# Last attention of a four-layer graph network: VectorE's weights and decays moved from SBUF to PSUM, row sums in six banks

## What is computed

```python
h = (x @ W_att).reshape(n, H, D)                 # H = 8, D = 64
a_src = jnp.einsum('nhc,hc->nh', h, att_src)
a_dst = jnp.einsum('nhc,hc->nh', h, att_dst)
e = a_src[src] + a_dst[dst]
e = jnp.where(e > 0, e, SLOPE * e)
m = jax.ops.segment_max(e, dst, num_segments=n)
e = jnp.exp(e - m[dst])
s = jax.ops.segment_sum(e, dst, num_segments=n)
alpha = e / (s[dst] + SM_EPS)
msg = alpha[:, :, None] * h[src]
out = jax.ops.segment_sum(msg, dst, num_segments=n)
```

## Time and profile before

| what | value |
|---|---|
| median of 3 runs | 5495.73 us (5489.99 to 5499.63) |
| the profiled execution's own time | 5500.16 us |
| its span, first to last instruction | 5498.4 us |
| POOL busy | 3629.3 us (66%) |
| DVE busy | 4024.2 us (73%) |
| PE busy | 2485.3 us (45%) |
| ACT busy | 1267.6 us (23%) |

### The profile page before, as it was taken

The page is one execution under the profiler, slowest core; times in us unless marked ns, Lnnn a source line. Parts: engine busy times, 40 slices in busy tenths (PEclk is TensorE's granted clock), DMA queues, the critical chain, the costliest instruction groups (busy, mean ns, idle before and its releaser), DMA issues.

```text
span 5498.4 us, 51371 instructions
## 1 busy us (share of the span) xinstructions
PE 2485.3 (45%) x13080; PEld 1698.2 (31%) x13080; DVE 4024.2 (73%) x7076; ACT 1267.6 (23%) x4432; POOL 3629.3 (66%) x3780
## 2 busy tenths in 40 slices
PE   1697100102112133333332335559882677777765
PEld 0572000101112123232232324537771233323324
DVE  9877888887886578787887878745552676677677
ACT  0000000000000011111111111110002777777761
POOL 2777777777777777777777777430006777777743
PEclk6555555555555555555555555569996888888886
DMA  7212111121222232323222233237761222222222
GB/s 251 56 54 58 49 55 46 48 71 42 62 53 66 50 82 80 83 79 83 75 79 82 80 83 89 79 97 254 235 200 30 76 86 86 78 85 86 79 73 67
DMA packets 392241, 476.93 MB, mean 87 GB/s; under 512 B 216403, under 2 KB 252309, under 8 KB 384838
## 3 DMA queue, kind: packets, MB, share of 16 engines
q1 hardware_dynamic: 136422, 279.67, 15.0%
q0 software_dynamic: 114832, 133.36, 10.7%
q10 hardware_dynamic: 140752, 61.28, 4.0%
HBM read 294.77 MB, written 179.24 MB: 86 GB/s over the span
## 4 chain that ended last, share of the span: by engine, by line
POOL 51%; issue 20%; DVE 15%; PE 9%; DMA 4%; ACT 0%; POOLq 0%; ACTq 0%; DVEq 0%; SPq 0%
POOL arena L794 36%; POOL rec_dram L751 12%; PE acc L2267 4%; DVE OHX L1547 3%; PE pw L2255 2%; DMA V<-in_edge_attr_dram 1%; DVE oh L1557 1%; DVE arena L1569 1%; DVE V L1589 1%; DVE arena L1573 1%; POOL own_dram L771 1%; DVE sc L1574 1%; DMA rec_dram<-V,rowst 1%; DVE oh L1547 1%; PE acc L2209 1%
## 5 line engine op out<-in xcount | busy, mean ns | idle before, releaser
L794 POOL DMA_INDIRECT arena<-tab_dram,jst x2592 | 2527.3, 975 | 778.6 <-issue 772.7
L751 POOL DMA_INDIRECT rec_dram<-V,rowst x784 | 840.3, 1072 | 231.4 <-issue 221.4
L2201 PE MATMUL pw<-OHX 128*128 128x128 bf16 x1632 | 207.7, 307 | 800.0 <-DVE OHX L1547 798.7
L2209 PE MATMUL acc<-arena,oh 128*128 128x64 f32 x1952 | 420.7, 415 | 254.0 <-DVE oh L1557 254.0
L2209 PEld LDWEIGHTS acc<-arena,oh 128*128 128x128 f32 x1952 | 410.9, 325 | 268.2 <-issue 268.2
L982 ACT ACTIVATE arena<-arena,ew 128x64 f32<-128x64 f32 x1728 | 417.8, 333 | 31.2 <-PE acc L2303 31.2
L982 ACT ACTIVATE OHX<-arena,ew 128x64 f32<-128x64 f32 x1728 | 417.8, 333 | 2.5
L2303 PE MATMUL acc<-OHX,ident 128*128 128x512 f32 x432 | 252.9, 751 | 364.2 <-ACT OHX L982 361.6
L2201 PEld LDWEIGHTS pw<-OHX 128*128 128x128 bf16 x1632 | 154.7, 139 | 850.7 <-DVE OHX L1547 850.7
L1569 DVE TENSOR_TENSOR arena<-arena,pt 128x1024 f32<-128x1024 f32 x108 | 131.9, 1221 | 386.4 <-DMA arena<-tab_dram,jst 384.3
L744 POOL TENSOR_TENSOR pdum<-pdum 128x1 f32<-128x1 f32 x197 | 53.4, 271 | 440.7 <-DVE arena L1844 199.2
(11 more groups left out here) (578 smaller groups left out, 6272.6 us busy)
## 6 DMA issues: line engine op xcount, KB each, us to landing
arena<-tab_dram,jst POOLq DMA_INDIRECT x2592
arena<-rec_dram SPq DMA_DIRECT2D x122, 288.0 KB, 3.7
mt_dram<-oh ACTq DMA_DIRECT2D x272, 128.0 KB, 1.7
rows_dram<-V SPq DMA_DIRECT2D x27, 1056.0 KB, 4.0
rows_dram<-arena SPq DMA_DIRECT2D x27, 1056.0 KB, 4.3
V<-in_edge_attr_dram ACTq DMA_DIRECT2D x97, 256.0 KB
oh<-mt_dram SPq DMA_DIRECT2D x42, 512.0 KB, 4.7
OHX<-mt_dram SPq DMA_DIRECT2D x38, 512.0 KB, 4.6
```

Of the source, the lines that this page charges most:

```text
L751: gp.indirect_dma_start(rec[:, :], bass.IndirectOffsetOnAxis(ap=rowst[:, q, k:k + 1], axis=0), recst[:, q, k, :], None).then_inc(S[f"scat{ ...
L794: gp.indirect_dma_start(hd.G[:, a.r, j, :], None, table[:, :], row_of(jst[:, a.r, j:j + 1])).then_inc(S[f"rows{a.r}"], 16)
L2201: last = nc.tensor.matmul(unit_bank(c.slot)[:, k // 2 * P:(k // 2 + 1) * P], mones[c.slot][:, 0, k, :], mones[c.slot][:, 1, k, :], start=k ...
L2209: last = nc.tensor.matmul(o, roh[:, c.q, k, :], RG[:, c.r, k, 0:D], start=False, stop=True, skip_group_check=True)
```

## The change

The weights that DVE uses (the first four edges of each pair of rows, 128 numbers a partition) and the decays (64 numbers) now stand in PSUM, in the two banks of `pt`, one for even and one for odd blocks. ACT writes them there: L973 puts its result there, and a new instruction takes the exponential of the 128 arguments a second time, ahead of the one over all 256 in SBUF, which ACT's own weighting and the sums of the weights still need; DVE's wait for `dx` counts one more. Block 26 keeps both in SBUF.

Since `pt` no longer holds row sums, rows 6 and 7 of a block use the banks of rows 2 and 3. So PE must have had rows 2 and 3 read before it sums pair 3 of the same block, and the states are made two pairs later in DVE's order relative to the pair they belong to, but partly inside their own block: after weighting pairs 0 and 1 come the states of pairs 2 and 3 of the block before, after weighting pairs 2 and 3 those of pairs 0 and 1 of the same block. Block 25 leaves only pairs 2 and 3 to the part outside the loop.

```diff
--- before.py
+++ after.py
@@ -526,7 +526,20 @@
 
         def row_bank(f):
 
-            return acc[:, f * 512:(f + 1) * 512] if f < 4 else (accw, pu, pt[:, 0:512], pt[:, 512:1024])[f - 4]
+            return (accw, pu)[f - 4] if 4 <= f < 6 else acc[:, f % 4 * 512:f % 4 * 512 + 512]
+
+        def last_block(a):
+
+            return isinstance(a.g, int) and a.g == NB3 - 1
+
+        def decays3(a):
+
+            return dc[:, a.q] if last_block(a) else pt[:, a.q * 512 + 128:a.q * 512 + 128 + RB * H3].rearrange("p (f h) -> p f h", h=H3)
+
+        def weights_of(a):
+
+            return (ew[:, a.q].rearrange("p (f k h) -> p f k h", k=8, h=H3)[:, :, 0:8 - VA] if last_block(a) else
+                    pt[:, a.q * 512:a.q * 512 + 128].rearrange("p (f k h) -> p f k h", k=8 - VA, h=H3))
 
         @block.sync
         def _(sp):
@@ -970,10 +983,14 @@
             def weights3(a):
 
                 act.wait_ge(S["de"], 2 * a.g + 1)
-                A.activation(dc[:, a.q], dc[:, a.q], ACT.Exp).then_inc(S["dx"], 1)
+                A.activation(decays3(a), dc[:, a.q], ACT.Exp).then_inc(S["dx"], 1)
                 act.wait_ge(S["de"], 2 * a.g + 2)
+                if not last_block(a):
+                    A.activation(weights_of(a), ew[:, a.q].rearrange("p (f k h) -> p f k h", k=8, h=H3)[:, :, 0:8 - VA], ACT.Exp
+                                 ).then_inc(S["dx"], 1)
+                    act.wait_ge(S["dx"], 3 * a.g + 2)
                 A.activation(ew[:, a.q], ew[:, a.q], ACT.Exp).then_inc(S["dx"], 1)
-                act.wait_ge(S["dx"], 2 * a.g + 2)
+                act.wait_ge(S["dx"], 3 * a.g + 2 + (not last_block(a)))
                 for f in range(RH):
                     slot_taken3(act, a, f)
                     for k in range(8 - VA, 8):
@@ -1860,8 +1877,8 @@
                     before = SO3[1 - half][:, RH - 1] if row == 0 else SO3[half][:, row - 1]
                     o = SO3[half][:, row]
                     byh = lambda u: u[:, 0:H3 * D].rearrange("p (h d) -> p h d", h=H3)
-                    st(V.tensor_tensor(byh(o), byh(before), dc[:, c.q, f].unsqueeze(2).to_broadcast([P, H3, D]), ALU.mult), wait=False)
-                    st(V.tensor_tensor(o[:, 512:520], before[:, 512:520], dc[:, c.q, f], ALU.mult))
+                    st(V.tensor_tensor(byh(o), byh(before), decays3(c)[:, f].unsqueeze(2).to_broadcast([P, H3, D]), ALU.mult), wait=False)
+                    st(V.tensor_tensor(o[:, 512:520], before[:, 512:520], decays3(c)[:, f], ALU.mult))
                     v.wait_ge(S["dsm"], RH * c.g + f // 2 + 1)
                     V.tensor_tensor(o[:, 0:512], o[:, 0:512], row_bank(f), ALU.add).then_inc(S["dpb"], 1)
                     v.wait_ge(S["dpb"], RB * c.g + f + 1)
@@ -1879,8 +1896,7 @@
                     t = f * 8 + k
                     ins = V.tensor_tensor(V3r[vslot[f]][:, k * 512:(k + 2) * 512].rearrange("p (k h d) -> p k h d", h=H3, d=D),
                                           G3[:, a.r, t:t + 2, 0:D].unsqueeze(2).to_broadcast([P, 2, H3, D]),
-                                          ew[:, a.q, t * H3:(t + 2) * H3].rearrange("p (k h) -> p k h", h=H3).unsqueeze(3)
-                                          .to_broadcast([P, 2, H3, D]), ALU.mult)
+                                          weights_of(a)[:, f, k:k + 2].unsqueeze(3).to_broadcast([P, 2, H3, D]), ALU.mult)
                     if k + 2 < 8 - VA:
                         st(ins)
                     else:
@@ -1895,7 +1911,7 @@
                                        own.unsqueeze(2).to_broadcast([P, RB, RK, H3]), ALU.add))
                     st(V.scalar_tensor_tensor(sc[:], sc[:], SLOPE, sc[:], ALU.mult, ALU.max))
                 scores(heads3, a, st, summed)
-                v.wait_ge(S["dx"], 2 * a.g + 2)
+                v.wait_ge(S["dx"], 3 * a.g + 2 + (not last_block(a)))
                 st(V.tensor_reduce(rden_[:, a.q].rearrange("p (f h) -> p f h", h=H3), ew[:, a.q].rearrange("p (f k h) -> p f h k", k=RK, h=H3),
                                    AX, ALU.add))
 
@@ -1903,13 +1919,17 @@
 
                 st = Steps(v, "dc", 22, a.g)
                 begin3(a, st)
-                sums = Steps(v, "ds", 24, c.g) if c else None
+                own, carry = Steps(v, "ds", 24, a.g), Steps(v, "ds", 24, c.g) if c else None
+                if c:
+                    carry.k = 12
                 for pair in range(RH):
-                    if c:
-                        states3(c, sums, pair)
                     weighted3(a, pair, st)
-                assert st.k == 22
-                assert not c or sums.k == 24
+                    if pair >= 2:
+                        states3(a, own, pair - 2)
+                    elif c:
+                        states3(c, carry, pair + 2)
+                assert st.k == 22 and own.k == 12
+                assert not c or carry.k == 24
             blocks(v, NB3 - 1, block3)
 
             Xm, d_, b_, X_, CT, resets = CX3
@@ -1917,7 +1937,8 @@
             four = lambda u: u.rearrange("p (j n) -> p j n", n=P)
             final, ahead = [Group(t // 4, t % 4) for t in (NB3 - 1, NB3 - 2)]
             sums = Steps(v, "ds", 24, ahead.g)
-            for pair in range(RH):
+            sums.k = 12
+            for pair in (2, 3):
                 states3(ahead, sums, pair)
             link(V.tensor_copy(four(resets), rmc[:, 0:P].unsqueeze(1).to_broadcast([P, 4, P])))
             link(V.tensor_tensor(XB[:], Hn[:], lnb[:, 0, :].unsqueeze(1).to_broadcast([P, NC, D]), ALU.add))
@@ -2296,9 +2317,7 @@
                 for f in range(RH):
                     pe.wait_ge(S["dvd"], RH * a.g + f + 1)
                     pe.wait_ge(S["dva"], RH * a.g + f + 1)
-                    after(pe, S["dpb"], RB * (a.g - 1) + 2 * f + 2)
-                    if f == RH - 1 and isinstance(a.g, int) and a.g == NB3 - 1:
-                        pe.wait_ge(S["dcx"], 1)
+                    after(pe, S["dpb"], RB * a.g - (6, 0, 2, -4)[f])
                     for k in range(8):
                         last = nc.tensor.matmul(row_bank(2 * f + k // RK), ident[:], V3r[vslot[f]][:, k * 512:(k + 1) * 512],
                                                 start=k % RK == 0, stop=k % RK == RK - 1)
```

## The result

The changed kernel takes 5460.58 us (median of 4 runs, 5456.45 to 5462.83), the kernel before beside it 5495.87 (4 runs, 5489.99 to 5499.63). The ratio is 0.9935, with a 95% interval of 0.992 to 0.995: **35.3 us or 0.65% faster**. The forecast was 5452, in a range of 5442 to 5470. Medians are of fast runs alone: one of e8's six runs, 5598.29 us at a lower granted clock, was a slow one. The profiled execution is the fastest of its four (5456.45), 4.1 us under their median, while that of the kernel before was 4.4 us over its own; so the two profiles lie 8.5 us further apart than the medians.

The account below looks back on a forecast made before the run. POOL's gathers alone were taken to bound the last attention, 49 us of them lengthening by VectorE. Operands in PSUM -44.1, ACT's exponential +0.3, new order 0: -43.8 from 5495.7 gives 5452 us, range 5442 to 5470.

Parts of the forecast that it names:

- A gather waits for a VectorE instruction with two SBUF inputs: Last attention, blocks 0 to 25: a gather starting during such an instruction ends 0.8 us after it; 49 us of lengthening.
- whoever starts first holds the shared ports to its end: Rule quoted from the Trainium skill for VectorE instructions with two SBUF inputs beside GpSimd; the prediction says its rows agree.
- The term of -44.1 us: Blocks 0 to 25: operands in PSUM end the gathers' lengthening beside L1880, L1863 and L1864, 40.5 + 3.6 us.
- Beside L1880: 54 gathers, 40.5 us. Beside L1863 and L1864: 29 gathers, 3.6 us: Blocks 0 to 25 before the change: lengthening above 0.946 us by VectorE instruction, the weighting L1880 and the decays' products.
- What stays stands beside L1910: Blocks 0 to 25 after the change: gathers over 0.96 us stand beside L1910; 3.1 + 1.1 + 0.9 us left.
- the rival of a smaller gain: Blocks 0 to 25: other two-input instructions take the gathers' place; gain 28 us instead of 44, median 5468; 8%.
- VectorE's own time: Large products with the new PSUM operand cost nothing extra: 687 ns with a PSUM input against 692 with two from SBUF.
- ACT's exponential: Extra exponential into PSUM before the weighting, 263 ns: hidden in blocks 0 to 24, +0.3 us in block 25.
- The new order at cost 0: New order of states and banks, blocks 0 to 25: 1.7 us of slack; VectorE still waits about 3 us for gathers.
- SP's stores move with the states and are waited for a block later: Stores of the states, last attention: part of the new order's step, counted at cost 0.
- The clock: Rival: PE's new wait lengthens its pauses, the attention's sums run at the low clock; +390 us, 5886; 3%.
- The median: Whole kernel: 43.8 us gained, from 5495.7 to 5452 us, 0.8% less; a gain of 35 to 51 us at 86%.

Follow-up runs that it names:

- e8: The changed kernel with 24 added matmuls behind the attention and 16 ahead of the feed-forward part, their results unread; 5457.46 us, ratio 0.9924 to the kernel before.
- e2: The changed kernel with the decays back in SBUF, only VectorE's weights in PSUM; 5503.18 us, ratio 0.9998 to the kernel before.
- e1: The changed kernel's new order and banks, but weights and decays both read from SBUF, without the extra exponential; 5502.14 us, ratio 0.9994 to the kernel before.
- e0: The changed kernel again, unaltered; 5468.41 us, ratio 0.9935 to the kernel before.
- e11: The changed kernel a third time, unaltered, in another group; 5450.80 us, ratio 0.9929 to the kernel before.
- e6: The kernel before with 16 added matmuls, their results unread, ahead of the feed-forward part's transposes; 5499.74 us, ratio 0.9999 to the kernel before.
- e3: The changed kernel with the weights back in SBUF and no extra exponential, only the decays in PSUM; 5518.23 us, ratio 1.0027 to the kernel before.
- e4: The changed kernel with SP waiting for both halves of a block's states before issuing either store; 5457.48 us, ratio 0.9929 to the kernel before.
- e7: The changed kernel with the scores, from VectorE's second instruction on them, also in PSUM in blocks 0 to 25; 5453.73 us, ratio 0.9915 to the kernel before.
- e10: The changed kernel with scores in PSUM too and 16 added matmuls ahead of the feed-forward part; 5443.53 us, ratio 0.9914 to the kernel before.

## Why the prediction was right, and where it was off

**A gather waits for a VectorE instruction with two SBUF inputs: right.** The changed profile has L1897 beside 200 gathers and none of them longer than the rest, e2's rows show held and free gathers of one block by their operands alone, and e1 excludes the order. Of the prediction's "whoever starts first holds the shared ports to its end", with which it has the rows agree, they show one half: in the earlier trace rows the gather starts first or together and VectorE's pair loses 0.04 us, not the 0.94 of the gather. The Trainium skill, "SBUF — State Buffer", section "Who interferes with whom", infers that a `tensor_tensor` does not stall descriptor generation; by that the change would have brought 0, and 789.40 against 836.86 us decides against it a second time.

**The term of -44.1 us: right in size, and its split by instruction not a price list.** The stage shrank by 47.6 us in the profile after, 43.9 in e0 and 46.9 in e11; part of the spread is the 2.2 us by which an unhindered gather differs between executions. The term itself, the lengthening over 0.96 us, fell by 45.0, 43.2 and 44.6 us. e6, whose attention is that of the kernel before, has a stage 2.7 us shorter (1089.7), so against it the three are 44.9, 41.2 and 44.2. The mean gather is 0.949 us (forecast 0.953). The step "Beside L1880: 54 gathers, 40.5 us. Beside L1863 and L1864: 29 gathers, 3.6 us" is true of that trace, and whoever had read it as the worth of each edit would have kept the decays in SBUF: in e2 the lengthening falls by 2.5 us in place of 40.5, and in e3 it grows by 11.6 in place of falling by 3.6 (medians 1.7 us faster, which can't be told from none, and 13.3 slower). The sum came out because both went at once.

**What stays stands beside L1910: half right.** Of the 4.2 us over 0.96, L1910 and L1912 have 1.9, and 1.5 stand beside L1558, the subtraction before the weights' exponential; it is one more instruction with two SBUF inputs, and the cadence, moved, meets it more often (4.6 of the 8.6 us in e8). This was the rival of a smaller gain; against the 5.1 us that the forecast left, it added 3.5 at most (e8) where the rival had 16.

**VectorE's own time: right.** 687 for 692 ns, 1221 for 1225 ns. The 62 cycles more for a PSUM source, an estimate of 65 ns from the table in the section on the TRN2 errata of the page "VectorE: DVE Perf Modes" of the Trainium skill, do not show. **ACT's exponential:** 281 ns against a forecast of 263, and the exponential of the decays went from 256 to 228 with PSUM as its target. Both are hidden until block 25, and block 25 to block 26 takes 50.6 us, 0.9 under the forecast of 51.5, for PE's pair 0 was shorter there (8.74 us against 9.62).

**The new order at cost 0: right for VectorE and PE, wrong for SP.** VectorE waits for the gathers 3.4 us a block (about 3 forecast), PE's last pair starts as ACT's weighting ends (5172.24), four pairs of block 25 run from 5228.24 to 5258.83, under 31 us. Block 25 landed at 5215.4 and not near 5221: 4.0 us of that lie before the stage, 3.5 in it, and the late landing takes 1.8 back. The step that failed is "SP's stores move with the states and are waited for a block later": who waits for a store was asked, not what it runs beside. It now runs beside the one landing with no cover, and costs **1.8 us** (1.7 in e0 and 1.6 in e11, from lags of 3.3 and 3.1 us).

**The clock: the rival was right in kind, wrong in place.** It looked for PE's low clock in the sums, where it turned up only in single pairs; the 6 us came in the feed-forward part, which the sum had no term for. With the new order and no added matmuls the tail was 188.2, 188.2 and 181.9 us in three executions of one program, and 182 to 191 in e1 to e4 and e7 (the eight matmuls at 7.19 us in e1, 4.8 and 5.2 in e2 and e3, 3.88 in e4 and e7); before it was 182.1 in the one profile. Whether the new order makes the low clock there more frequent, or one profile of before is too few to see it, stays open.

**The median.** 35.3, 36.5 and 41.4 us in three groups against 43.8. The profiled executions, from the stage's first gather to the end, are 40.3, 36.6 and 46.3 us shorter than that of the kernel before. The medians are 8.5, 7.3 and 2.4 us short of the forecast gain, and the two losing terms make 7.8, 7.7 and 1.3 us in the one profile of each group (landing 1.8, 1.7 and 1.6; tail 6.0, 6.1 and -0.3). That fits, but it isn't shown: a profile is one execution of several, the runs of a group lie 6 to 24 us apart, and the three profiled executions differ by up to 3.7 us in the stage alone.

## What to carry to other kernels

A list of stalls by cause, read from one trace, is a sum and not a price list: where a stall sets the phase of what is stalled, removing one cause alone can hand its hits to the next, so remove the causes together. The share of the period that a part's instructions fill prices it better than the trace does, but it is no bound: look also whether the time from the end of one hold to the next start is near the pause between two such instructions, for then nearly every one is met (25 us by the share, 39.6 measured). When an edit moves a transfer, ask also what it now runs beside, above all at the last landing of a stage, where nothing hides it.

## What the runs showed of the hardware

- A store of 1056 KB issued 1.0 us before the end of a block's last gather delays its landing by 1.8 us (lag 3.35 us against 1.54), issued 1.9 us before by 1.3 (2.85, e10), 2.9 us before by 0.5 (2.00, e7), 6.0 us before by nothing (1.55, e1).
- The time of a gather beside a VectorE instruction that was already running with two SBUF inputs is fixed by that instruction's end plus 0.8 us, whether it is the 1.24 us weighting or the 0.69 us product of e2; with its output in PSUM it holds all the same (L1917 in e7). In all traces of this stage the gathers that start up to 0.03 us after such an instruction take their usual time, and it is VectorE that gives way (0.49 us in place of 0.43 for L1915 in e7, 1.27 in place of 1.23 for L1880 before); those that start 0.05 us after it or later are held.
- One program's matmuls ran at either clock level in the same place in different executions: 3.88 and 7.19 us for the same eight; 16 matmuls of 128 columns that compute nothing ahead of them gave 3.97 to 3.98.
- An exponential of 128x64 from SBUF into PSUM takes 228 ns, into SBUF 256; one of 128x128 from SBUF into PSUM 281 ns.
